# Retention in a one-core decoder layer: ScalarE takes the row normalisation and the v copies, VectorE's row moments move to the end of the batch, and rows are turned between the first two score groups

## What is computed

```
xn = (x - mean) / sqrt(var + 1e-5)                  # over the 256 columns of a row
q, k, v = split(xn @ W_qkv)                          # 16 heads of 16 columns
ret = (q @ k.T) * decay                              # decay[h, t, s] = gamma[h] ** (t - s) for t >= s, else 0
r   = ret @ v + 256 * (q @ past_kv)
x   = x + group_norm(r)                              # mean and variance over heads, columns and rows of one batch
```

## Time and profile before

| | us |
|---|---|
| median of 3 runs | 1977.79 |
| lowest, highest run | 1969.37, 1978.92 |
| the profiled execution | 1959.3 |
| its span, from first to last instruction | 1957.5 |
| PE busy, DVE busy, ACT busy, POOL busy | 1794.8, 1476.9, 1200.5, 545.8 |

### The profile page before, as it was taken

One profiled execution on the slowest core, in us unless ns is written; L12 is line 12 of the kernel. 1 busy time (PEld: TensorE's weight loads), 2 busy tenths in 40 slices (PEclk: granted clock), 3 DMA queues, 4 the chain that ended last, 5 costly groups with the idle time before them and its releaser, 6 DMA issues. The chain is left out here.

```text
span 1957.5 us, 36131 instructions
## 1 busy us (share of the span) xinstructions
PE 1794.8 (92%) x12564; PEld 967.1 (49%) x12564; DVE 1476.9 (75%) x3037; ACT 1200.5 (61%) x2439; POOL 545.8 (28%) x654
## 2 busy tenths in 40 slices
PE   6788776699999999999999999999999998789999
PEld 5667665334444444443444444444344433357875
DVE  6787874698888888888788888888878886475345
ACT  3122213067878877887777787787787778625540
POOL 2101102233142214303314221430431100036675
PEclk9889897589999999999999999999999999989999
DMA  6000004712630632533173062253217200154564
GB/s 196 1 2 1 2 1 103 124 35 72 119 69 2 157 72 31 119 72 69 64 127 68 2 157 58 45 116 75 69 58 133 35 2 2 40 172 146 173 195 129
DMA packets 67427, 152.14 MB, mean 78 GB/s; under 512 B 12384, under 2 KB 39008, under 8 KB 67104
## 3 DMA queue, kind: packets, MB, share of 16 engines
q1 hardware_dynamic: 60432, 131.20, 28.8%
q0 software_dynamic: 6816, 18.62, 3.4%
HBM read 95.82 MB, written 53.23 MB: 76 GB/s over the span
## 5 line engine op out<-in xcount | busy, mean ns | idle before, releaser
L1285 DVE TENSOR_REDUCE x_mx<-x_ps 128x1 f32<-128x512 f32 x1536 | 974.4, 684 | 190.4 <-PE x_ps L1011 182.1
L1182 ACT ACTIVATE x_probs<-x_ps 128x512 f32<-128x512 f32 (+1 forms) x1664 | 894.6, 597 | 271.5 <-PE x_ps L1075 269.0
L1075 PE MATMUL x_ps<-x_qst,x_kst 50*128 50x512 f32 (+1 forms) x1664 | 591.0, 451 | 24.2 <-ACT x_probs L1182 23.7
L1011 PE MATMUL x_ps<-x_kst,x_qst 48*128 48x512 f32 x1536 | 574.1, 459 | 17.8 <-ACT x_kp L1133 11.4
L1059 PE MATMUL x_ps<-x_probs,x_vst 128*17 128x512 f32 (+1 forms) x3328 | 443.2, 605 | 4.8 <-ACT x_ou L1159 4.8
L1011 PEld LDWEIGHTS x_ps<-x_kst,x_qst 48*128 48x128 f32 x1536 | 240.7, 189 | 400.9 <-DVE x_mx L1285 281.6
L1075 PEld LDWEIGHTS x_ps<-x_qst,x_kst 50*128 50x128 f32 (+1 forms) x1664 | 240.8, 182 | 112.4 <-ACT x_probs L1182 104.4
L1823 POOL DMA_INDIRECT f_xt<-rows_x,f_ids x78 | 78.3, 1004 | 232.4 <-DVE f_ids L2000 194.5
L1211 POOL TENSOR_TENSOR x_vst<-x_kp,x_bv 128x320 f32<-128x320 f32 x32 | 27.7, 867 | 390.3 <-ACT x_kp L1133 354.6
L861 POOL TENSOR_TENSOR x_kp<-x_rest,x_zero 128x256 fp32r<-128x256 f32 (+1 forms) x105 | 59.6, 568 | 245.3 <-ACT x_rest L1153 179.8
L1059 PEld LDWEIGHTS x_ps<-x_probs,x_vst 128*17 128x17 f32 (+1 forms) x3328 | 55.2, 95 | 134.9 <-issue 70.3
(11 more groups left out here) (233 smaller groups left out, 2451.8 us busy)
## 6 DMA issues: line engine op xcount, KB each, us to landing
x_kst<-k_parts SPq DMA_DIRECT2D x192, 200.1 KB, 8.6
k_parts<-x_kp SPq DMA_DIRECT2D x16, 1601.0 KB, 5.4
x_kp<-in_ctxT SPq DMA_DIRECT2D x8, 1601.0 KB, 7.4
x_qst<-q_parts SPq DMA_DIRECT2D x192, 64.0 KB, 2.3
sorted_y<-f_yt SPq DMA_DIRECT2D x26, 384.0 KB
q_parts<-x_qp SPq DMA_DIRECT2D x8, 1024.0 KB, 4.3
x_all<-in_x SPq DMA_DIRECT2D x8, 512.0 KB, 3.8
rows_x<-f_xn SPq DMA_DIRECT2D x8, 512.0 KB, 8.1
```

What stands on the lines that cost most here:

```text
L1011: m = pe.matmul(o, qst[mg][rows, pair, t * P:(t + 1) * P], kst[mg][rows, pair, i * 512:(i + 1) * 512], start=True, stop=True)
L1075: pe.matmul(ps[0:w, n % S_BANKS, :], kst[g][rows, pair, c * P:c * P + w], qst[g][rows, pair, :], start=True, stop=True).then_inc(s_filled, 1)
L1182: nc.scalar.activation(probs[0:w, s % (2 * GH), :], ps[0:w, s % S_BANKS, :], ACT.Exp, scale=HD ** -0.5).then_inc(exp_done, 1)
L1285: nc.vector.tensor_reduce(out=mx[:, 2 * pair + half, t, i:i + 1], in_=o, axis=AX.X, op=ALU.max).then_inc(drained_v, 1)
```

## The change

ACT gets three new steps: `root_rows` (the root of the row variance), `normalise_rows` (four activations with scale 1/std and bias -mean/std) and `keep_v` (v from PSUM to `vz`, after DVE has made kd from the same bank, counted by a semaphore `v_kept`, on which PE waits where it reuses a v bank and before the first state). DVE's `values` keeps only kd. DVE's `normalise_moments` is for the rows two batches ahead, with tiles of its own, and stands between `states(b, 2)` and `output(b, 2)`; `scale_rows` (a reciprocal and a `scalar_tensor_tensor` for the bias) stands between `output(b, 2)` and `output(b, 3)`. On all engines and in `r_items` the turned rows come between scores 0 and scores 1. Declarations of tiles and semaphores are left out:

```diff
@@ -62
     out = [[("out", b, c)] for c in range(TT)]
-    return ([("v", b, c) for c in range(TT)] + score(0) + score(1) + ahead("xnT") + state(0) + out[0] + score(2) + ahead("q")
+    return ([("v", b, c) for c in range(TT)] + score(0) + ahead("xnT") + score(1) + state(0) + out[0] + score(2) + ahead("q")
             + state(1) + out[1] + score(3) + ahead("k") + state(2) + out[2] + out[3])
@@ -70
          for n, last in enumerate(R_STREAM)]
-R_ROOTS = [("norm", 0)] + [root for b in range(B) for root in (
-    [("norm", b + 1)] * (b < B - 1) + [("batch", b - 1), ("second", b - 1)] * (b > 0))] + [("batch", B - 1), ("second", B - 1)]
+R_ROOTS = [(kind, b) for b in range(B) for kind in ("batch", "second")]
@@ -189
                 if n >= R_BANKS:
-                    wait_drained(pe, R_STREAM[n - R_BANKS])
+                    last = R_STREAM[n - R_BANKS]
+                    wait_drained(pe, last)
+                    if last[0] == "v":
+                        pe.wait_ge(v_kept, last[1] * TT + last[2] + 1)
                 return n % R_BANKS
@@ -261
                     wait_drained(pe, ("v", b, TT - 1))
+                    pe.wait_ge(v_kept, (b + 1) * TT)
                 for f in range(KT):
@@ -294
                 scores(b, 0)
-                scores(b, 1)
                 if b < B - 1:
                     turn_rows(b + 1)
+                scores(b, 1)
                 states(b, 0)
@@ -338
+            def root_rows(b):
+                act.wait_ge(rows_var, b + 1)
+                nc.scalar.activation(nstd[:], nvar[:], ACT.Sqrt).then_inc(rows_std, 1)
+            def normalise_rows(b):
+                act.wait_ge(rows_scaled, b + 1)
+                for t in range(TT):
+                    ins = nc.scalar.activation(xn[:, t, :], x_all[:, b * TT + t, :], ACT.Identity,
+                                               bias=nmr[:, t:t + 1], scale=nrstd[:, t:t + 1])
+                ins.then_inc(xn_ready, 1)
+            def keep_v(b, c):
+                wait_drained(act, ("v", b, c))
+                nc.scalar.activation(vz[:, c, :, 0:4:3, :], read(act, "v", b, c)[:, D:2 * D].rearrange(
+                    "p (h x d) -> p h x d", x=2, d=HD), ACT.Copy).then_inc(v_kept, 1)
             def round_rows(b):
@@ -358
                 if b < B - 1:
-                    root("norm", b + 1)
+                    normalise_rows(b + 1)
+                keep_v(b, 0)
+                keep_v(b, 1)
                 if b:
                     root("batch", b - 1)
+                keep_v(b, 2)
+                keep_v(b, 3)
                 if b < B - 1:
@@ -374
                 keep_out(b, 2)
+                if b < B - 2:
+                    root_rows(b + 2)
                 keep_out(b, 3)
-            root("norm", 0)
+            root_rows(0)
+            normalise_rows(0)
             act.wait_ge(rw_loaded, 16)
             keep_k(0)
+            act.wait_ge(vz_zero, 1)
+            root_rows(1)
             for b in range(B):
@@ -445
                 dve.wait_ge(x_loaded, b * 16 + 16)
-                row_moments(b)
-            def normalise(b):
-                dve.wait_ge(std_ready, root_no("norm", b))
-                link(nc.vector.reciprocal(rstd[:], std[:]))
                 for t in range(TT):
-                    ins = nc.vector.tensor_scalar(xn[:, t, :], x_all[:, b * TT + t, :],
-                                                  lmv[:, t, 0:1], rstd[:, t:t + 1], ALU.subtract, ALU.mult)
-                ins.then_inc(xn_ready, 1)
+                    ins = nc.vector.bn_stats(nbst[:, t, :], x_all[:, b * TT + t, :])
+                link(ins)
+                if b:
+                    dve.wait_ge(rows_scaled, b)
+                for t in range(TT):
+                    ins = nc.vector.bn_aggr(nlmv[:, t, :], nbst[:, t, :])
+                link(ins)
+                if b:
+                    dve.wait_ge(rows_std, b)
+                nc.vector.tensor_scalar(nvar[:], nlmv[:, :, 1], EPS, None, ALU.add).then_inc(rows_var, 1)
+            def scale_rows(b):
+                dve.wait_ge(rows_std, b + 1)
+                if b:
+                    dve.wait_ge(xn_ready, b)
+                link(nc.vector.reciprocal(nrstd[:], nstd[:]))
+                nc.vector.scalar_tensor_tensor(out=nmr[:], in0=nlmv[:, :, 0], scalar=-1.0, in1=nrstd[:],
+                                               op0=ALU.mult, op1=ALU.mult).then_inc(rows_scaled, 1)
@@ -505
                 o = read(dve, "v", b, c)
-                nc.vector.tensor_tensor(kd[:, c, :], o[:, 0:D], kscale[:], ALU.mult)
-                nc.vector.tensor_copy(vz[:, c, :, 0:4:3, :], o[:, D:2 * D].rearrange(
-                    "p (h x d) -> p h x d", x=2, d=HD)).then_inc(drained_v, 1)
+                nc.vector.tensor_tensor(kd[:, c, :], o[:, 0:D], kscale[:], ALU.mult).then_inc(drained_v, 1)
@@ -538
                     batch_moments(b - 1)
-                if b < B - 1:
-                    normalise_moments(b + 1)
                 values(b, 0)
                 values(b, 1)
-                if b < B - 1:
-                    normalise(b + 1)
                 if b:
@@ -565
                 states(b, 2)
+                if b < B - 2:
+                    normalise_moments(b + 2)
                 output(b, 2)
+                if b < B - 2:
+                    scale_rows(b + 2)
                 output(b, 3)
             normalise_moments(0)
-            normalise(0)
+            scale_rows(0)
             keep_xnT(0)
@@ -579
             ins.then_inc(past_ready, 1)
-            dve.wait_ge(vz_zero, 1)
+            normalise_moments(1)
+            scale_rows(1)
             for b in range(B):
```

More of the change, by code:

```diff
@@ L128, in retention @@
         gs2 = sb("r_gs2", [P, 2])
+        nbst = sb("r_nbst", [P, TT, 6])
+        nlmv = sb("r_nlmv", [P, TT, 2])
+        nvar, nstd = sb("r_nvar", [P, TT]), sb("r_nstd", [P, TT])
+        nrstd, nmr = sb("r_nrstd", [P, TT]), sb("r_nmr", [P, TT])
         var = sb("r_var", [P, TT])
@@ L142, in retention @@
         xn_ready, past_ready = sem("xn_ready"), sem("past_ready")
+        rows_var, rows_std, rows_scaled, v_kept = sem("r_rows_var"), sem("r_rows_std"), sem("r_rows_scaled"), sem("r_v_kept")
         q_wide, q_decayed = sem("q_wide"), sem("q_decayed")
```

## The result

The first comparison gave 1937.0 us (median of 4; 1926.32 to 1950.59) against 1973.58 before: ratio 0.9884, interval 0.9837 to 0.9932. The forecast was 1945.4 in a range of 1933 to 1957. The profiled executions lie only 18 us apart, 1941.3 against 1959.3 us (spans 1939.5 and 1957.5). Where the time went shows in two steps. Behind retention the profiled execution after takes 14 us longer, though the code there is the same.

The account below looks back on a forecast made before the run. DVE's queue was taken to set the front of each retention batch. Batches 1 to 6 gain 30.2 us, start 1.6, batch 7 0.6: 32.4 in sum, giving 1945.4 us in a range of 1933 to 1957.

Parts of the forecast that it names:

- Front of the batch: From the batch statistics to the first score: 4.74 us leave DVE, first score 3.64 us after instead of 7.64, gain 4.0.
- ACT has room: ACT takes over normalisations and v copies within its waits and those of PE, at cost 0.
- Back of the batch: Moments and the row scaling fit into DVE's waits for outputs 2 and 3: cost 0, 0.8 us to spare.
- Rival 2: POOL holds the new `scalar_tensor_tensor` at the back of the batch: 6.3 us lost, 1951.7 us; chance 0.07.
- Turned rows: First score to `states(b, 0)`: turned rows between scores 0 and 1 cut 7.10 us to 6.07, gain 1.03.
- Rival 1: TensorE at half clock for scores 1: 5.6 us later, outputs up to as much again, 1951 to 1956; chance 0.18.
- other bound: In retention, without slow clock after the long wait: 0.42 us more per batch, 2.5 more in all, 1943 us.
- Start: First projection at about 15.0 us rather than 16.64, as ACT normalises and POOL splits later: gain 1.6 us.
- Batch 7: Last batch, no next rows, loses only its copies: 4.23 us down to 3.64, gain 0.6.
- Rival 4: Cross-attention at a lower granted clock after denser retention: slower, 1988 us if 85 us run at 1.2 GHz; chance 0.05.

Follow-up runs that it names:

- Experiment 5: The four v copies put back on DVE in the kernel after, cut after retention: 291.61 us.
- Experiment 6: Row moments, bias and scale of the next rows put back in the front of the batch in the kernel after, cut after retention: 304.0 us.
- experiment 3: Turned rows put back behind scores 1 in the kernel after, cut after retention: 282.65 us.
- 4: Only the turned rows moved between scores 0 and 1 in the kernel before, cut after retention: 317.71 us.
- first profile: The first profiled execution of the whole kernel after, unchanged: 1941.3 us, span 1939.5.
- third profile: A later profiled execution of the whole kernel after, no edit, in a round measuring 1929.87 us; profile span 1928.4 us.
- the second: A later profiled execution of the whole kernel after, no edit, in a round measuring 1937.14 us; profile span 1922.6 us.
- retention alone: Kernels before and after cut after retention, without cross-attention and feed-forward: 316.55 us before, 284.42 after.
- both of 8: POOL's two steps exchanged and turned rows behind scores 1 again, in the kernel after: 277.05 us cut after retention, 1933.69 whole.

## Why the prediction was right or wrong

- **Front of the batch, 4.0 us: right.** 3.67 us measured for 3.64, with the wait for v3 (0.51 for 0.6). Experiment 5 shows that a step counts by what DVE's queue has left over PE's, not by its length: 1.33 us of copies are worth 0.56 where the clock stays up. Copies (7 us) and moments (20) were undone one at a time; the normalisations alone were not, so their share is only argued.
- **ACT has room: right.** The v copies are 0.38 long, and no wait for one of its new steps ends last in the followed batch. Experiment 6 shows where the room ends: the normalisations have to be done before the root of the batch variance is wanted, or DVE waits for it (0.81 us).
- **Back of the batch, nothing: right.** The new `scalar_tensor_tensor` (L501) is 0.16 long at 111.62; POOL starts its operation at 112.31, 0.7 later. Rival 2 did not happen.
- **Turned rows, 1.03 us: the size right, the cause wrong.** The step that failed is "from the first score to `states(b, 0)`": it gave the gain to the new order. The time did fall by 0.94 us, but experiments 3 and 4 show that the order is worth nothing either way, and batch 7 loses the wait without it. Of the wait of 1.03 us, 0.94 was scores 1 at half clock (2.09 for 1.15) behind PE's wait of 4.34, and the shorter front removed it by itself. That the size fitted is luck: the new order was to hide the wait, and there was no longer any to hide. A gain that two edits could bring had been booked to one, without asking what the row would be with the other alone.
- **Rival 1 (half clock): in some batches.** Behind 1.71 us of waiting scores 1 took 1.15 every time, but in the first two batches of the first and of the third profile the products after them were slow (period 30.8 to 31.0, mean clock 0.94). The other two profiles of the kernel after, the second and that of retention alone, had no such batch; there a batch gains 5.3 us over the mean before, above the 5.03 forecast, which is the gain that this rival gave as its other bound.
- **Start, 1.6 us: mis-sized, from the rows of one execution.** The first projection began at 15.85 instead of 16.64, 0.8 us. POOL did hold `past_bd` to the end of its split, as forecast. In the third profile it began at 15.09, close to the 15.0 forecast; in the first the chain was 0.8 later, since the four-element L494 took 0.90 us at 6.72, beside POOL's presets, instead of 0.17. But the start before was no fixed 16.64 either. In the two profiles of retention alone with the old start it began at 14.02 and 13.83, 1.1 us and more before the new one: ACT waited 1.34 us for the weights' DMA, so POOL split them from 9.99, behind DVE's normalisations, which took 1.99 us and not the 5.14 of the earlier trace rows:

```profile
7.33 1.99 DVE L454 TENSOR_SCALAR r_xn<-x_all,r_lmv,r_rstd 128x256 f32<-128x256 f32 x4
```

  Whether the cut kernel or the single execution moved the weights' arrival is open. The term counts on a collision that does not happen every time.
- **Batch 7, 0.6 us: too small.** It lost 2.1 us (29.42 to 27.29): 0.5 in the front, 0.95 of the wait for scores 1, and the rest behind them, where PE's states took 1.22 us before (half clock) and 0.71 after. The prediction had left the wait of this batch as it was, though the earlier trace rows show its scores 1 at 2.09.
- **The sum and the clock.** 32.4 forecast, 32.1 in retention alone. That the profiled pair has 32.3 is in part luck. To the first statistics it gained 0.9 us (forecast 1.6), in batches 1 to 6 29.2 (forecast 30.2; two batches ran at the lower clock), in batch 7 2.1 (forecast 0.6). In the profiles of retention alone the same three are 0.2, 31.8 and 2.2, in all 34.1. The whole-time median fell by 36.6 in the first comparison, by 20 to 32 in the later ones. Rival 4 (the clock withheld later) explains the profiled pair, but as chance of an execution; a steady price of 14 us is excluded, one of up to 8 is not quite.

## What to carry to other kernels

When one engine's queue sets the front of a stage, price a moved step by what the next engine in line leaves of it: 4.74 us left the queue, 4.0 arrived. Before crediting a reordering with a gap, look at why the gap's other side is slow; a matmul group at twice its usual time behind a wait is a matter of TensorE's clock, and a shorter wait ahead of it may remove it (2.09 to 1.15 us here). Where the start depends on when a load lands, look at more than one execution. Where a later, untouched stage scatters by more than the gain, cut the kernel behind the changed stage: 32 us were plain in four executions of 300 us and blurred (30, give or take 6) in sixteen of 1950.

## What the runs showed of the hardware

- POOL's 2.38 us operation holds a one-element DVE operation with two inputs in SBUF until it ends: 1.26 us beside it (113.45 to 114.71, POOL's from 112.31 to 114.69), 0.21 without it. The Trainium skill ("SBUF — State Buffer", Who interferes with whom) describes such an exclusive hold for a VectorE instruction with two SBUF inputs beside a GpSimd one that reads SBUF, and the rows agree. A four-element `tensor_scalar` was also stretched, from 0.17 to 0.90 us, beside POOL's presets (`MEMSET`), which only write constants; in the third profile it took 0.17 beside the same presets.
- After PE's waits of 1.54 us the clock stayed at 2.4 GHz in all six batches of three profiles (experiment 3, and both of 8). After 1.71 us, in a batch with the turned rows done ahead of the wait, it fell to 1.2 GHz in some batches: two of six in two profiles of the kernel after, none in the other two. There scores 1 took 1.15 us and the products behind them were slow; with POOL's steps exchanged scores 1 themselves took 1.6 to 1.7 us in three batches. The wait alone does not decide: in experiment 5 scores 1 took 1.15 us behind 2.25 us of waiting in four batches of six, in batch 7 of the kernel before 2.09 behind 2.09.
- The last group of cross-attention, with the same 153 matmuls, ran at a granted clock of 1.00 in one execution and 0.72 in another of the same code (31.4 and 39.6 us, second and first profile of the kernel after).
